# Cross-attention with a second, image-like context on one core: first scores placed behind the Gram run, transposes of sums inside it, and the last text projection in two parts

## The reference, cut to what matters

```
q   = heads(x @ W_q);  k, v = heads(text @ W_k), heads(text @ W_v)
p_t = softmax(q @ k.T * 0.25)                    # 20 heads x 112 x 371
text_out = p_t @ v
s_ip = q @ heads(ip @ W_k_ip).T * 0.25           # 4 image tokens
qsem = l2norm(p_t @ text);  ip_n = l2norm(ip)    # in the 512-wide context
p_ip = softmax(s_ip + 0.5 * qsem @ ip_n.T) * mask
out  = (text_out + p_ip @ heads(ip @ W_v_ip)) @ W_out + b_out + x
```

## Time and profile before

| | us |
|---|---|
| three runs | 429.76, 431.2, 434.5 (median 431.2) |
| the profiled execution | 428.83 |
| its span | 427.0 |
| TensorE busy | 400.7 (94%) |
| weight loads busy | 323.6 (76%) |
| VectorE busy | 223.1 (52%) |
| ScalarE busy | 206.0 (48%) |
| GpSimd busy | 206.3 (48%) |
| granted TensorE clock, mean | 0.986 |

### The profile page before, as it was taken

One profiled execution on the slowest core, in us unless ns is written; L12 is line 12 of the kernel. 1 busy time (PEld: TensorE's weight loads), 2 busy tenths in 40 slices (PEclk: granted clock), 3 DMA queues, 4 the chain that ended last, 5 costly groups with the idle time before them and its releaser, 6 DMA issues.

```text
span 427.0 us, 9498 instructions
## 1 busy us (share of the span) xinstructions
PE 400.7 (94%) x3656; PEld 323.6 (76%) x3656; DVE 223.1 (52%) x482; ACT 206.0 (48%) x483; POOL 206.3 (48%) x218
## 2 busy tenths in 40 slices
PE   8999798999999999999999999999998899979985
PEld 5649678787888878887878797887886687856762
DVE  0893772765456635662656346653655166613432
ACT  1524135464555554656444645454554345537721
POOL 3020380353547643666259625764375225724881
PEclk9999998999999999999999999999999899989999
DMA  8599793057227220561147022722063000001000
GB/s 272 141 321 202 196 161 110 20 161 128 65 71 166 50 78 2 163 120 41 39 143 140 12 69 75 161 49 78 2 138 71 12 28 3 0 3 37 3 13 16
DMA packets 29455, 38.03 MB, mean 89 GB/s; under 512 B 14361, under 2 KB 26745, under 8 KB 28729
## 3 DMA queue, kind: packets, MB, share of 16 engines
q1 hardware_dynamic: 28514, 36.36, 35.2%
q10 hardware_dynamic: 896, 1.07, 0.9%
HBM read 28.50 MB, written 8.81 MB: 87 GB/s over the span
## 4 chain that ended last, share of the span: by engine, by line
PE 86%; DVE 5%; DMA 3%; issue 2%; SPq 2%; POOL 1%; ACT 1%; DVEq 0%; POOLq 0%
PE PR L895 40%; PE Y L895 26%; PE P L895 10%; PE O L895 8%; DMA qst<-ma 2%; SPq L457 1%; DVE mx L797 1%; PE PR L1053 1%; DMA big<-xT 1%; DVE big L763 1%; POOL pb L544 1%; DVE pb L819 0%; ACT cTs L719 0%; DVE Gl L789 0%; PE PR L1058 0%
## 5 line engine op out<-in xcount | busy, mean ns | idle before, releaser
L544 POOL TENSOR_TENSOR pb<-pb 128x448 f32<-128x448 f32 x78 | 89.0, 1141 | 128.9 <-DVE pb L819 123.5
L797 DVE TENSOR_REDUCE mx<-PR 112x1 f32<-112x371 f32 x160 | 83.8, 540 | 77.6 <-PE PR L895 77.1
L819 DVE TENSOR_TENSOR pb<-big,Y 128x448 f32<-128x448 f32 x120 | 73.1, 620 | 52.9 <-PE Y L895 52.7
L895 PE MATMUL Y<-er,Gh 128*128 128x448 f32 x240 | 97.4, 406 | 0.8 <-DVE pb L819 0.6
L895 PE MATMUL Y<-er,Gl 128*128 128x448 f32 x240 | 89.1, 371 | 0.0
L678 ACT ACTIVATE big<-P 128x448 f32<-128x448 f32 x120 | 65.3, 544 | 29.6 <-PE P L895 28.9
L682 ACT ACTIVATE er<-big 128x448 fp32r<-128x448 f32 x120 | 69.3, 578 | 3.8
L895 PEld LDWEIGHTS Y<-er,Gh 128*128 128x128 f32 x240 | 46.3, 193 | 14.1 <-DVE pb L819 10.0
L895 PE MATMUL PR<-kst,qst 96*112 96x371 bf16 x160 | 51.2, 331 | 3.0 <-DVE mx L797 1.8
L895 PE MATMUL P<-qst,kst 99*128 99x112 bf16 x480 | 42.3, 214 | 8.5 <-DMA qst<-ma 8.5
L895 PEld LDWEIGHTS P<-qst,kst 99*128 99x128 bf16 x480 | 29.8, 99 | 24.9 <-issue 18.2
(11 more groups left out here) (147 smaller groups left out, 660.6 us busy)
## 6 DMA issues: line engine op xcount, KB each, us to landing
et<-ctxT SPq DMA_DIRECT2D x8, 752.0 KB, 4.5
kst<-kd SPq DMA_DIRECT2D x7, 720.0 KB, 7.2
kd<-ks SPq DMA_DIRECT2D x16, 288.0 KB, 2.9
qst<-qd SPq DMA_DIRECT2D x48, 70.0 KB, 2.5
kst<-kd SPq DMA_DIRECT2D x7, 480.0 KB, 9.2
kst<-kd SPq DMA_DIRECT2D x9, 240.0 KB, 9.3
qd<-kst SPq DMA_DIRECT2D x4, 336.0 KB, 5.7
vx<-xr SPq DMA_DIRECT2D x8, 140.0 KB, 2.2
```

What stands on the lines that cost most here:

```text
L544: pool.tensor_tensor(total, total, (pz, pm)[j], ALU.add).then_inc(s_S, 1)
L797: dve.tensor_reduce(mx[b % 2][:, h:h + 1], bank[0:S, 0:T], AX.X, ALU.max).then_inc(s_free[seq[u] % NR], 1)
L819: dve.tensor_tensor((pz, pm, pa[g % 2])[j], eb[g % 3][:, 448 * j:448 * j + 448], Y[y % 2][:, 0:448], ALU.mult).then_inc(s_P, 1)
L895: return pe.matmul(o, st, mv, start=start, stop=stop, **kw)
```

## The change

It changes the order of units, and the form of the last projection:

- The last round of batches 5 and 6: `p g pT v S0 cT S1 S2 o`. Of batch 0: `E g v S0 S1 S2`.
- Round 2 of batches 1 to 6: T0 and T1 stand between the first Gram tile (`g2`) and the other two.
- Start of batch 0: `G 1 2` ahead of the first `St`; K 2 0 between the second and third `St`; in round 0 the K units and maxima in another order.
- Batch 7, fourth round: `p` stands ahead of S1 and `g1`.
- Tail: `cT` is split. The first 128 columns of the text sums (complete with the first twelve heads) are transposed in a unit `cT0` of its own, into bank `Y0`, and copied by ScalarE; `vWo` and `ot` are each in two parts that alternate. The transposes use the transpose form instead of matmuls with the identity.

The diff, its tables shown in a few lines:

```diff
--- before.py
+++ after.py
@@ -50,19 +50,19 @@
 
 ROUNDS = ("S0 K0 m g m K1 S1 m v S2 m G0 m",
           "S0 m g m K2 m S1 v m S2 G1 m",
-          "S0 m T0 T1 g m r0 G2 m S1 m pw v S2 m V0",
+          "S0 m g2 T0 T1 g1 g0 m r0 G2 m S1 m pw v S2 m V0",
           "Kr S0 r1 m g m V1 m S1 m m v r2 S2 mT z V2",
           "p E g pT v cT S0 S1 o S2")
-EARLY = ("K0 S0 m g m S1 K1 S2 m m m",
+EARLY = ("m S0 m K1 g m S1 m S2 m",
          "S0 m g m S1 K2 m S2 v m m",
          "S0 m g m S1 m v S2 V0 m m",
          "Kr S0 m g m V1 m S1 m m v S2 mT V2",
-         "E g2 g1 S0 g0 S1 v S2")
-LATE = "p S0 g2 g1 pT g0 S1 v cT S2 o"
+         "E g v S0 S1 S2")
+LATE = "p g pT v S0 cT S1 S2 o"
 LAST = ("S0 g2 S1 g1 g0 S2 v T0 T1",
         "S0 r0 pw g2 S1 g1 g0 S2 v",
         "S0 r1 g2 S1 g1 r2 g0 S2 v",
-        "S0 z g2 S1 g1 p g0 S2 v pT T0'",
+        "S0 z g2 p S1 g1 g0 S2 v pT T0'",
         "g2 cT r0' pw' g1 o g0 r1' v vW r2' z' p'")
 
 
@@ -86,7 +86,7 @@
     side = spread(side, [("max", 0, h) for h in range(H)])
     cut = side.index(("qip", 3))
     order += side[:cut] + split(2) + side[cut:]
-    order += [("mT", 0), ("G", 1, 0), ("G", 1, 1), ("St", 0, 0), ("G", 1, 2), ("St", 0, 1), ("St", 0, 2)]
+    order += [("mT", 0)] + [("G", 1, i) for i in range(3)] + [("St", 0, 0), ("St", 0, 1), ("K", 2, 0), ("St", 0, 2)]
     for b in range(B):
         n, f = b + 1, b - 1
         maxes = iter([("max", n, h) for h in range(H)])
@@ -123,7 +123,8 @@
                 elif w in unit:
                     order.append(unit[w])
     b = B - 1
-    order += [("pv", NG * B - 1), ("T", b, 1), ("vWo", b), ("end", 0), ("pw", b, 1), ("cT", b), ("ot", b), ("end", 1), ("z", b, 1), ("end", 2)]
+    order += [("pv", NG * B - 1), ("T", b, 1), ("cT0", b), ("vWo", b, 0), ("end", 0), ("pw", b, 1)]
+    order += [("cT", b), ("ot", b, 0), ("vWo", b, 1), ("ot", b, 1), ("end", 1), ("z", b, 1), ("end", 2)]
     order += [("pT", b), ("o", b)]
     return order
 
@@ -312,6 +313,8 @@
         s_pTs = sem("s_pTs")
         s_cTs = sem("s_cTs")
         s_vp = sem("s_vp")
+        s_cp = sem("s_cp")
+        s_ca = sem("s_ca")
         s_va = sem("s_va")
         s_xb = sem("s_xb")
         s_fin = sem("s_fin")
@@ -707,12 +710,19 @@
                     for c, w in enumerate(CW):
                         last = act.activation(vrT[0:w, c, :], P[1][0:w, 80 * c:80 * c + 80], ACT.Copy)
                     last.then_inc(s_va, 1)
-                elif k == "ot":
+                elif k == "vWo" and u[2] == 1:
                     act.wait_ge(s_vp, 2)
                     act.activation(vrWo, P[0][0:80, 0:C], ACT.Copy).then_inc(s_va, 1)
                 elif k == "pT":
                     filled(act, u)
                     act.activation(pTs[:, :], bank[0:80, 0:S], ACT.Copy).then_inc(s_free[seq[u] % NR], 1)
+                elif k == "cT0":
+                    act.wait_ge(s_cp, 1)
+                    act.activation(cTs[:, 0, :], Y[0][:, 0:S], ACT.Copy).then_inc(s_ca, 1)
+                elif k == "cT" and u[1] == B - 1:
+                    filled(act, u)
+                    act.activation(cTs[:, 1, :], bank[:, S:2 * S], ACT.Copy)
+                    act.activation(cTs[0:64, 2, :], bank[0:64, 2 * S:3 * S], ACT.Copy).then_inc(s_free[seq[u] % NR], 1)
                 elif k == "cT":
                     filled(act, u)
                     act.activation(cTs[:, 0:2, :], bank[:, 0:2 * S].rearrange("p (c s) -> p c s", c=2), ACT.Copy)
@@ -1056,18 +1066,29 @@
                     b = u[1]
                     pe.wait_ge(s_p, b + (2 if b == B - 1 else 1))
                     pe.transpose(bank[0:80, 0:S], pe_[:, :, :].rearrange("p h n -> p (h n)"), ident[0:S, 0:S]).then_inc(s_ring, 1)
+                elif k == "cT0":
+                    b = u[1]
+                    pe.wait_ge(s_P, 3 * NG * B)
+                    pe.wait_ge(s_tn, b + 1)
+                    t = tn[:, :, :].rearrange("p h d -> p (h d)")
+                    pe.transpose(Y[0][:, 0:S], t[:, 0:128], ident[0:S, 0:S]).then_inc(s_cp, 1)
+                elif k == "cT" and u[1] == B - 1:
+                    b = u[1]
+                    pe.wait_ge(s_tn, b + 2)
+                    t = tn[:, :, :].rearrange("p h d -> p (h d)")
+                    for c in (1, 2):
+                        last = pe.transpose(bank[0:CW[c], S * c:S * c + S], t[:, 128 * c:128 * c + CW[c]], ident[0:S, 0:S])
+                    last.then_inc(s_ring, 1)
                 elif k == "cT":
                     b = u[1]
                     pe.wait_ge(s_vb, b + 1)
-                    pe.wait_ge(s_tn, b + (2 if b == B - 1 else 1))
-                    if b < B - 1:
-                        freed(pe, seq[("pT", b)])
+                    pe.wait_ge(s_tn, b + 1)
+                    freed(pe, seq[("pT", b)])
                     t = tn[:, :, :].rearrange("p h d -> p (h d)")
                     for c in range(3):
                         o = bank[0:CW[c], S * c:S * c + S]
-                        last = mm(o, t[:, 128 * c:128 * c + CW[c]], ident[0:S, 0:S], True, b == B - 1)
-                        if b < B - 1:
-                            last = mm(o, vr[b % 2][:, 128 * c:128 * c + CW[c]], pTs[:, :], False, True)
+                        mm(o, t[:, 128 * c:128 * c + CW[c]], ident[0:S, 0:S], True, False)
+                        last = mm(o, vr[b % 2][:, 128 * c:128 * c + CW[c]], pTs[:, :], False, True)
                     last.then_inc(s_ring, 1)
                 elif k == "vW":
                     b = u[1]
@@ -1079,15 +1100,19 @@
                 elif k == "vWo":
                     b = u[1]
                     pe.wait_ge(s_va, 1)
-                    for c in range(3):
+                    for c in ((0, 1), (2,))[u[2]]:
                         last = mm(P[0][0:80, 0:C], vrT[0:CW[c], c, :], wo_s[0:CW[c], c, :], c == 0, c == 2)
-                    last.then_inc(s_vp, 1)
+                    if u[2]:
+                        last.then_inc(s_vp, 1)
                 elif k == "ot":
-                    b = u[1]
+                    b, part = u[1], u[2]
                     n = seq[("o", b)]
-                    freed(pe, n - NR)
-                    freed(pe, seq[("cT", b)])
-                    for c in range(3):
+                    if part == 0:
+                        freed(pe, n - NR)
+                        pe.wait_ge(s_ca, 1)
+                    else:
+                        freed(pe, seq[("cT", b)])
+                    for c in ((0,), (1, 2))[part]:
                         mm(PR[n % NR][0:S, 0:C], cTs[0:CW[c], c, :], wo_s[0:CW[c], c, :], c == 0, False)
                 elif k == "o" and u[1] == B - 1:
                     b = u[1]
```

## The result

| | before | after |
|---|---|---|
| median, us | 430.48 (4 runs, 429.19 to 434.5) | 411.81 (4 runs, 411.41 to 413.53) |
| profiled execution, us | 428.83 | 411.41 |
| its span, us | 427.0 | 409.6 |
| mean granted clock | 0.986 | 0.997 |

The ratio is 0.956, with an interval of 0.949 to 0.963. A second comparison, of 5 rounds, gave 413.68 us (6 runs, 412.11 to 414.71) against 430.66 (11 runs), a ratio of 0.961 with an interval of 0.958 to 0.965. From here on the spans of profiled executions are compared; they differ by 17.4 us, where my sum had 15.7. Lines of the helper and of the engines' loops have moved: L895 is now L905, L1053 is L1063, L1058 is L1068.

A forecast was written before the change was run, and what follows sets the result against it. TensorE, with 86% of the chain, bounds the kernel, so only its standstills and half-clock stretches pay. Terms 9.3 + 4.0 + 1.5 - 0.4 + 0.8 + 0.5 = 15.7 us; forecast 415.0 us, range 411.5 to 421.5.

The forecast's parts named there:

- first scores, batches 5 and 6: Last rounds of batches 5 and 6: waits for maxima and half-speed stretches behind them go, 9.3 us won.
- transposes of sums: Round 2, batches 1 to 6: Gram matmuls cover the six waits for VectorE's eviction, 4.0 us won.
- start of batch 0: Batch 0's start: shorter waits and no half speed, partly given back to VectorE and ScalarE, 1.5 us won.
- end of batch 0: Batch 0's last round: ScalarE's 1.1 us per score tile sets the pace, 0.4 us lost.
- `p` and the tail: Last batch: `pe_` ready earlier, 0.8 us won; last text projection in two parts, 0.5 us won.
- Rival A: At each batch change ScalarE is the gate, costing a tile (1.1 us) in batches 5 and 6: 418 us; chance 0.12.
- B: At the transposes of sums the bank wait returns through a late copy of R: 419 us; chance 0.06.
- C: Half clock does not depend on the removed waits; three stretches come back elsewhere: 420 us; chance 0.09.
- D: Transposes inside Gram runs or short pieces at batch changes bring half clock, slower than before: about 442 us; chance 0.02.
- E: The maxima come later because their DMAs wait behind something new, only 4 to 6 us won: 426 us; chance 0.05.

The follow-up runs named there:

- the kernel with the fill: Changed kernel with the old last round in batches 5 and 6, plus 14 unread matmuls ahead of the wait for the maxima: 420.61 us, ratio 0.980.
- the kernel with both new orders: Changed kernel with K 2 0 ahead of batch 0's first score, and batch 0's last-round sums between first and second score: 411.77 us, ratio 0.955.
- the kernel after once more: The changed kernel measured again in five rounds, nothing changed: 413.68 us, ratio 0.961.

## Which steps of the prediction held, and which failed

Of the six parts of the sum four came as forecast. Two steps failed. The price of the transposes' wait was mis-sized: 4.0 us in the sum, 6.36 measured. And the new start of batch 0 does not win what it was said to: 1.5 us in the sum, -0.27 by the test with the old order.

| term | predicted | by the traces |
|---|---|---|
| first scores, batches 5 and 6 | 9.3 | 9.8 (4.95 + 4.85) |
| transposes of sums | 4.0 | 6.36 |
| start of batch 0 | 1.5 | 1.27 |
| end of batch 0 | -0.4 | -0.37 |
| `p` and the tail | 0.8 + 0.5 | 0.67 + 0.49 |
| start of the program | 0 | -0.84, not from the change |
| sum | 15.7 | 17.4 |

*First scores.* Right, and by the mechanism named: the waits went whole, nothing came late behind them (ScalarE's `er` was ready for the next Gram run, the gap for `cTs` is 0.18 us), and the clock followed, as the kernel with the fill shows. That the two stretches are no accident of one profile can be read from the mean clocks: in 35 further timed executions of the kernel before, none is above 0.990, which is what two stretches of 3.4 us and the last 2 us leave of 427; kernels with the new order reach 0.999. Rival A, ScalarE as the gate, happened only at the end of batch 0, where the forecast had it. The size was 0.5 us short for the reason of the next point: waits of 3.08 and 2.95 us were worth 3.36 and 3.20.

*Transposes of sums.* The mechanism was right, the size was not, and this is the step that made the sum too small: "Term: 4.0 us. Bounds: 0, if the wait turns up again at the next bank user, and 4.9". I took the list of waits for the price. Start to start the maximum and the transposes are 0.98 us apart, and with the wait gone 1.06 us a batch came back, so six times that is above the upper bound too. I had written it in the section on the profile myself, that the time from start to start is what a matmul costs.

*Start of batch 0.* The number came out near, but by luck. The steps were "with 0.3 us of standstill left I take it as gone", of the stretch from 70.0 to 73.4 (it is gone, but it was absent with the old order as well, in the one execution of it that was profiled) and "That fills 1.2 of the 1.4 us". K 2 1's wait on VectorE (0.79 us in the list, where I had 0.9; at 73.20 and not at 72.3, since `mT` 0 itself stands 0.84 us later in this execution) and the one for `er` (0.84, where I had 1.3) gave back all that the shorter waits had won. By the test with the old start the term is -0.27 us, close to the lower bound of -0.3, which I had set for another reason (half speed stays).

*Start of the program.* TensorE waited 1.33 us for the first weights `wq` in the profiled execution of after, and not in that of before; its first matmul behind them starts 0.96 us later. In the kernel with both new orders this wait is 0.54 us, in the kernel after once more there is none.

*End of batch 0.* As forecast, in size and in its two gaps behind ScalarE.

*`p` and the tail.* As forecast. T 7 0 waits for OT, 0.37 us in the list and 0.53 from start to start, and the last `pT` still waits for `pe_`.

*Rivals.* B costs nothing in this position and 0.29 us a batch one tile later. C, the half clock elsewhere: none in this execution, and nine of the twelve later ones have at least one ahead of 75 us; the two at the batch changes did not come back in any kernel that has the new order there. But the early ones are no price of the change. The mean clocks say how long an execution ran at half clock in all (what the mean lacks to 1, times the span, times two): 12.6 us on average in those 35 of the kernel before, 4.8 in the 44 of kernels with the new order at the batch changes. The difference of 7.8 us is the two stretches (6.8) and 1.0 more, which is not clear of the scatter. The four executions of the kernel with the old start of batch 0 alone ran 4.7 us at half clock on average, no more than the others. D, half clock from the transposes, fell: all twelve executions with the transposes inside the Gram run, the one with them a tile later among them, show 1.00 in batches 1 to 4. The Trainium skill (TensorE: Matmul & The Clock Gate, "Part 4: PE-mode transpose") says that a transpose does not count as activity in the way a matmul does; no run here shows an effect of it. E fell: the last of the DMAs for the maxima is issued 3.07 us behind `mT` 6 before and 3.09 after.

*The level.* The forecast was a gain of 16.2 us from the median of before (431.2 to 415.0). By the medians it is 18.7 us in the first comparison and 17.0 in the second. The 2.36 us on the transposes is the largest part of what it missed. The difference between the two comparisons is taken as scatter, of the kind told of next. The low end of the range was too high by the terms themselves: I had put it at the lowest run less 18 us, while the upper bounds of the six terms add up to 19.7 (410.1).

## What the runs showed of the clock

I had expected half clock only behind long standstills. In 14 profiled executions (before, after twice, and 11 others), leaving out the end of the span, it came as follows, each time for 3.4 us (the windows above cut off 0.1 us):

| what TensorE did before | times seen | half clock began within 2 us |
|---|---|---|
| waited 2.9 to 3.1 us, batches 5 and 6 | 4 | 4 |
| the same 3 us filled with matmuls | 2 | 0 |
| waited 1.84 us for a maximum, at 50 us | 14 | 3 |
| waited 1.7 to 1.9 us, batches 5 and 6 | 2 | 1 |
| waited 1.4 us, start of batch 0 | 2 | 1 |
| waited 0.73 us ahead of `mT`, at 64 us | 14 | 4 |
| no wait in the list, at 31 us, loads running | 14 | 3 |
| waited 0.79 to 1.2 us, other places behind 70 us | 26 | 0 |
| all else behind 75 us, waits under 0.75 us | 14 executions | 0 |

Behind the waits of 3 us it began 0.3 to 1.0 us after TensorE was at work again; of the four at `mT`, two began up to 0.1 us before the wait of 0.73 us ended. Ten of the 14 executions have such a stretch in their first 75 us, one of them two, always at one of these places. It costs up to 1.8 us: from the first `P<-big,pb` matmul (at 6.4 to 7.6 us) to `mT` 0 it is 56.3 to 57.2 us without one and 57.8 to 58.1 with. The times of a kernel's runs go with it: of the 35 executions of the kernel before, the seven at a mean clock of 0.990 took 428.1 to 429.4 us, the two at 0.979 took 434.0 and 434.6. So medians of four runs could not tell 1 us. The Trainium skill (TensorE: Matmul & The Clock Gate, "What's actually happening") says that the throttled clock is the default and activity releases it; the waits of 3 us and their filled counterpart agree with it. The stretches at 31 us have no standstill of TensorE over 0.15 us in the 10 us ahead of them that would explain them. What decides in the cases that go both ways stays open; no run was made on it.

## What to carry to other kernels

A wait in the middle of an in-order queue is priced from start to start, between two instructions that both kernels have, and not by the idle time that a list names: here 0.66 us in the list was 1.06 us, six times over. A long standstill of TensorE costs a second time through its clock (1.6 us behind each of 3 us here), so it is the first to be covered with work that is ready, and a few matmuls that nobody reads show at once which part is the clock's. Before a stretch of half clock in one profile is put into a sum, look whether it comes back in a second execution: the one at 70 us made a term look right whose order was worth -0.27 us.
